# Expert tiles of 128 rows with one gather each, one summed number per list place, and earlier sums in a two-layer Flamingo block

## What is computed

```python
def _L0_ffn_ref(x, Wg, W1, W2):            # x: 4096 tokens of 128
    cap = max(1, T // E)                   # 512
    probs = jax.nn.softmax(xt @ Wg, axis=-1)
    _, top_idx = jax.lax.top_k(probs.T, cap)          # each expert takes its best 512
    ...
    tok2exp = jnp.where(assigned, jnp.argmax(masked, axis=0), jnp.argmax(pT, axis=0))
    for e in range(E):                     # each token is used by exactly one expert
        gate = jnp.where(tok2exp == e, weights, 0.0)
        out = out + gate[:, None] * (gelu(xt @ W1[e]) @ W2[e])      # 128 -> 256 -> 128
...
x = x + tanh(g_xattn[0]) * _L0_xattn_ref(_layernorm(x), ctx_1024, ctx_1024, ...)
x = x + tanh(g_ffn[0])   * _L0_ffn_ref(_layernorm(x), ...)
x = x + tanh(g_xattn[1]) * _L1_xattn_ref(_layernorm(x), ctx_1024, ...)
x = x + tanh(g_ffn[1])   * _L1_ffn_ref(_layernorm(x), ...)   # top 2 of 8, 128 -> 512 -> 128
```

## Time and profile before

| | us |
|---|---|
| median of 3 runs | 759.71 |
| lowest and highest | 758.35, 764.55 |
| the profiled execution, whole time | 760.45 |
| its span (first to last instruction) | 758.6 |
| first attention | about 0 to 216 |
| first experts: routing and list | about 216 to 275 |
| first experts: tiles | 275 to 345 |
| second attention, with its last scatters | 348 to 578 |
| second experts | 580 to 736 |
| the end | 736 to 758 |

### The profile page before, as it was taken

One profiled execution on the slowest core, in us unless ns is written; L12 is line 12 of the kernel. 1 busy time (PEld: TensorE's weight loads), 2 busy tenths in 40 slices (PEclk: granted clock), 3 DMA queues, 4 the chain that ended last, 5 costly groups with the idle time before them and its releaser, 6 DMA issues.

```text
span 758.6 us, 16969 instructions
## 1 busy us (share of the span) xinstructions
PE 539.6 (71%) x5534; PEld 435.7 (57%) x5534; DVE 502.7 (66%) x1605; ACT 358.3 (47%) x830; POOL 315.0 (42%) x439
## 2 busy tenths in 40 slices
PE   0699999998721039872699988888403999999940
PEld 0466777776510028761466756665302999999940
DVE  5568888887358862222699999998561556655625
ACT  0246777776633014330167766677402555555510
POOL 6212222221200057743755227456772455555440
PEclk9959999999955558996599999999755999999985
DMA  8443334332000004362556546241123222222229
GB/s 262 153 136 92 101 109 115 107 88 66 16 14 1 0 21 97 99 84 66 146 163 185 163 135 190 84 121 53 40 64 101 61 69 71 79 72 72 65 70 296
DMA packets 100532, 74.50 MB, mean 98 GB/s; under 512 B 12928, under 2 KB 94592, under 8 KB 100160
## 3 DMA queue, kind: packets, MB, share of 16 engines
q1 hardware_dynamic: 92336, 55.17, 25.5%
q0 software_dynamic: 7040, 14.56, 7.6%
q10 hardware_dynamic: 1072, 3.70, 1.4%
HBM read 43.64 MB, written 31.39 MB: 99 GB/s over the span
## 4 chain that ended last, share of the span: by engine, by line
PE 41%; DVE 22%; issue 11%; POOL 10%; DMA 8%; ACT 5%; SPq 2%; ACTq 1%; POOLq 0%; DVEq 0%
PE bank L943 10%; PE bank L953 10%; DVE MX L1089 7%; PE bank L740 5%; POOL PT L582 5%; PE bank L766 4%; PE bank L887 4%; PE bank L754 3%; POOL dispatched L556 3%; DVE PT L1285 2%; DMA PT<-normed,LIST 2%; PE bank L842 1%; ACT XT_HL_WR L654 1%; DMA QS_N<-MH 1%; ACT OT L678 1%
## 5 line engine op out<-in xcount | busy, mean ns | idle before, releaser
L623 ACT ACTIVATE PT<-bank 128x512 f32<-128x512 f32 x256 | 151.8, 597 | 95.1 <-PE bank L754 93.9
L1089 DVE TENSOR_REDUCE MX<-bank 128x4 f32<-128x512 f32 x256 | 172.1, 681 | 25.9 <-PE bank L766 24.2
L766 PE MATMUL bank<-KS,QS_N 96*128 96x128 f16 x1024 | 104.5, 228 | 16.7 <-DVE MX L1089 8.7
L593 POOL DMA_INDIRECT returned<-PT,META_ROW x78 | 74.9, 961 | 84.6 <-DVE PT L1403 72.4
L953 PEld LDWEIGHTS bank<-WALL,HT 128*128 128x128 f32 x808 | 100.9, 194 | 5.1 <-issue 1.7
L953 PE MATMUL bank<-WALL,HT 128*128 x808 | 102.1, 278 | 0.6 <-issue 0.6
L943 PE MATMUL bank<-XGT,XT_HL_WR 128*128 128x256 f32 x404 | 101.9, 392 | 0.0
L766 PEld LDWEIGHTS bank<-KS,QS_N 96*128 96x128 f16 x1024 | 76.6, 103 | 43.4 <-DVE MX L1089 15.3
L754 PE MATMUL bank<-QS_N,KS 98*128 98x512 f16 x256 | 98.0, 388 | 1.8 <-DMA QS_N<-MH 1.6
L943 PEld LDWEIGHTS bank<-XGT,XT_HL_WR 128*128 128x128 f32 x404 | 75.0, 198 | 8.0
L556 POOL DMA_INDIRECT dispatched<-N,SLOT x64 | 64.3, 1004 | 30.0 <-issue 14.1
(11 more groups left out here) (210 smaller groups left out, 917.4 us busy)
## 6 DMA issues: line engine op xcount, KB each, us to landing
spread<-XT_HL_WR SPq DMA_DIRECT2D x96, 128.0 KB, 2.0
QS_N<-spread SPq DMA_DIRECT2D x128, 48.0 KB
KS<-spread SPq DMA_DIRECT2D x32, 192.0 KB
PT<-dispatched SPq DMA_DIRECT2D x39, 132.0 KB, 2.1
WALL<-in_w SPq DMA_DIRECT2D x8, 578.0 KB
CT<-in_ctx SPq DMA_DIRECT2D x32, 128.0 KB
returned<-PT SPq DMA_DIRECT2D x23, 128.0 KB, 2.2
WALL<-in_w ACTq DMA_DIRECT2D x1, 2048.0 KB, 8.5
```

The lines of the kernel that those rows point to most:

```text
L593: pool.indirect_dma_start(ys[1][:, :], bass.IndirectOffsetOnAxis(ap=META_ROW[:, a.f, c:c + 1], axis=0), YS[:, a.f, c, :], None).then_inc(S ...
L623: nc.scalar.activation(PT[:, c, 4 * g:4 * g + 4, :].rearrange("p j q -> p (j q)"), ST[i % 2][:, :], ACT.Exp, scale=SCALE[layer]).then_inc( ...
L766: last = nc.tensor.matmul(MB[i % 2][:, j * P:(j + 1) * P], QS[0:96, m.r, J * g + j, c * P:(c + 1) * P], KS[0:96, m.r, g, c * P:(c + 1) * P ...
L1089: V.tensor_reduce(out=MX[:, m.u, 2 * J * g + c:2 * J * (g + 1):2], in_=MB[i % 2][:, :].rearrange("p (j k) -> p j k", j=J), op=ALU.max, axi ...
```

## The change

- The first layer's tiles have 128 slots instead of 256 (`SIZE = (P, TILE)`): 4096/128 + 7 = 39 tiles and 39 blocks. Each tile takes one gather; the same `XG` memory now is six buffers of 128 rows. Transposes, copies, products, gelu and the result's copy and write are made for 128 columns. The second layer's tiles keep 256.
- The list sums one number per place instead of two. Tokens are numbered 32 p + b, the number less 2048 fits float16, and one DVE instruction makes `IDS`; POOL's and ACT's parts and one of the two joining instructions are gone. `POS` is made in parts of 12, 8, 8 and 4 batches. A place without a token now gets 2048.
- Because tokens are numbered 32 p + b, `normed` and `returned1` are laid out in that order, and the loads at the end read 8 neighbouring rows (4096 bytes) per partition.
- In the second attention the results are gathered and added earlier: pairs 0 and 1 ahead of the slots, then by the table `GATHERS`, and added by the table `SUMS_AT` (slot, position in the slot): 1, 1, 2 and 3 pairs in slots -4 to -1, four in slot 0, four in slot 1, one in slot 2. Before it was one pair in each of the slots -4 to 11.
- `starts` compares the counts with 32 steps instead of 16, and `tables(0)` is made for 39 tiles instead of 23.

```diff
+SIZE = (P, TILE)
+TILES = (T // P + E - 1, 2 * T // TILE + E - 1)
+BLOCKS = TILES[0]
...
+PARTS = (0, 12, 20, 28, 32)
+GATHERS = {-4: (2, 3), -3: (4, 5), -2: (6, 7, 8), -1: (9, 10, 11), 0: (12, 13, 14), 1: (15,)}
+SUMS_AT = {(-4, 0): 0, (-3, 0): 1, (-2, 0): 2, (-2, 5): 3, (-1, 0): 4, (-1, 2): 5, (-1, 5): 6, (0, 1): 7, (0, 3): 8, (0, 4): 9, (0, 6): 10,
+           (1, 1): 11, (1, 2): 12, (1, 4): 13, (1, 6): 14, (2, 1): 15}
...
+    rows = (B * p + np.arange(B)[None, :]).astype(np.int32)
...
         XG = PT[:, 0].rearrange("p h q -> p (h q)")[:, 0:6 * ROW].rearrange("p (u c w) -> p u c w", u=3, c=2)
+        XG6 = XG[:, :, :, :].rearrange("p u c w -> p (u c) w")
...
-                    sp.dma_start(normed[y.b * P:(y.b + 2) * P, :].rearrange("(c p) d -> p c d", p=P),
+                    sp.dma_start(normed.rearrange("(p b) d -> p b d", b=B)[:, y.b:y.b + 2, :],
...
-                    sp.dma_start(ys[0][i * TILE:(i + 1) * TILE, :].rearrange("(c p) d -> p c d", p=P), YS[:, a.f, :, :]).then_inc(SO[a.f], 16)
+                    sp.dma_start(ys[0][i * P:(i + 1) * P, :], YS[:, a.f, 0, :]).then_inc(SO[a.f], 16)
...
-                    y = ys[1].rearrange("(b p) d -> p b d", p=P)
-                    sp.dma_start(N[:, b, 0:D], y[:, B + 8 * k:B + 8 * k + 8, :]).then_inc(YL[k], 16)
-                    sp.dma_start(N2[:, b, 0:D], y[:, b, :]).then_inc(YL[k], 16)
+                    first, second = (ys[1][T * c:T * (c + 1), :].rearrange("(p b) d -> p b d", b=B) for c in range(2))
+                    sp.dma_start(N[:, b, 0:D], second[:, b, :]).then_inc(YL[k], 16)
+                    sp.dma_start(N2[:, b, 0:D], first[:, b, :]).then_inc(YL[k], 16)
...
-                        for k in range(2 * p + 9, min(2 * p + 11, PAIRS)):
+                        for k in GATHERS[p] if p in GATHERS else ():
                             gather_results(Pair(1, k // 4, k % 4))
...
-                pool.wait_ge(own, 1)
-                nc.gpsimd.tensor_tensor(out=IDS[:, :, 1, :], in0=OWN[:, :, :], in1=const("batch").unsqueeze(2).broadcast_to([P, B, BLOCKS]),
-                                        op=ALU.mult).then_inc(ids_b, 1)
...
-                    if a.g >= 3:
-                        pool.wait_ge(xg_t, a.g - 2)
-                    for c in range(2):
-                        pool.indirect_dma_start(XG[:, a.t, c, 0:D], None, normed[:, :],
-                                                bass.IndirectOffsetOnAxis(ap=LIST[:, 2 * i + c:2 * i + c + 1], axis=0)).then_inc(XA[a.t], 16)
+                    if i >= 6:
+                        pool.wait_ge(xg_t, i - 5)
+                    pool.indirect_dma_start(XG6[:, i % 6, 0:D], None, normed[:, :],
+                                            bass.IndirectOffsetOnAxis(ap=LIST[:, i:i + 1], axis=0)).then_inc(XA[i % 6], 16)
...
-                gather_results(Pair(1, 0, 0))
+                for k in range(2):
+                    gather_results(Pair(1, 0, k))
...
-                    act.wait_ge(own, 1)
-                    nc.scalar.activation(IDS[:, :, 0, :], OWN[:, :, :], ACT.Copy, scale=const("partition")).then_inc(ids_p, 1)
...
+                        rows = (XG6[:, a.i % 6:a.i % 6 + 1, :], XG[:, a.t, :, :])[layer]
+                        for c in range(1 + layer):
+                            last = transpose(bank[4 + a.u][:, c * P:(c + 1) * P], rows[:, c, 0:D])
...
+                            n = SIZE[layer]
+                            last = nc.tensor.matmul(bank[2 * a.u + m // 2][:, n * (m % 2):n * (m % 2) + n],
+                                                    WR[:, a.t, m * P:(m + 1) * P], XGT[:, a.u, 0:n], start=True, stop=True)
...
-                        for c in range(2):
+                        for c in range(1 + layer):
                             for m in range(M):
...
+                    def add_result(u):
+                        if layer == 1 and (p, u) in SUMS_AT:
+                            k = SUMS_AT[p, u]
+                            k = Pair(1, k // 4, k % 4)
+                            dve.wait_ge(YGS[k.p % 8], 32 * (k.p // 8 + 1))
+                            for c in range(2):
+                                last = V.scalar_tensor_tensor(out=batch(k, c), in0=YG[:, k.p % 8, c, :], scalar=W0[:, k.b + c:k.b + c + 1],
+                                                              in1=batch(k, c), op0=ALU.mult, op1=ALU.add)
+                            last.then_inc(combined, 1)
...
-                    if n and layer == 1:
-                        dve.wait_ge(YGS[n.p % 8], 32 * (n.p // 8 + 1))
...
+                    add_result(0)
                     maxima(1)
                     if n:
+                        if layer == 1:
+                            dve.wait_ge(combined, n.p + 1)
...
                     routing(1)
+                    add_result(1)
                     maxima(2)
...
+                V.tensor_tensor(out=IDS[:, :, :], in0=OWN[:, :, :], in1=const("row_less_half").unsqueeze(2).broadcast_to([P, B, BLOCKS]),
+                                op=ALU.mult).then_inc(ids, 1)
+                for part in range(len(PARTS) - 1):
+                    b = slice(PARTS[part], PARTS[part + 1])
+                    n = PARTS[part + 1] - PARTS[part]
+                    V.tensor_tensor(out=POS[:, b, :], in0=const("places").unsqueeze(1).broadcast_to([P, n, P]),
+                                    in1=sm[5][:, b].unsqueeze(2).broadcast_to([P, n, P]), op=ALU.is_equal).then_inc(positions, 1)
...
-                link(V.tensor_copy(FIRST_IDS[:, :], PA[:, 0:BLOCKS]))
-                V.scalar_tensor_tensor(out=LIST[:, :], in0=PA[:, BLOCKS:2 * BLOCKS], scalar=float(P), in1=FIRST_IDS[:, :],
-                                       op0=ALU.mult, op1=ALU.add).then_inc(list_ready, 1)
+                V.tensor_scalar(out=LIST[:, :], in0=PA[:, 0:BLOCKS], scalar1=float(T // 2), scalar2=None, op0=ALU.add).then_inc(list_ready, 1)
...
-                        V.tensor_copy(YS[:, a.f, :, :].rearrange("p c d -> p (c d)"), bank[6 + a.u][:, 0:2 * D]).then_inc(y_kept, 1)
+                        V.tensor_copy(YS[:, a.f, 0, :], bank[6 + a.u][:, 0:D]).then_inc(y_kept, 1)
```

More of the change, by code:

```diff
@@ L175, in program @@
     ys = [nc.dram_tensor(f"returned{k}", [rows, D], F32, kind="Internal").ap()
-          for k, rows in enumerate((TILES[0] * TILE, PAD_ROW + T + 2 * E * TILE))]
+          for k, rows in enumerate((TILES[0] * P, PAD_ROW + T + 2 * E * TILE))]
     spread = nc.dram_tensor("spread", [2, 2, G, J, HD, 3, 2 * P], F16, kind="Internal").ap()
@@ L916, in expert_layer @@
                     rank()
-                    pe.wait_ge(ids_p, 1)
-                    pe.wait_ge(ids_b, 1)
+                    pe.wait_ge(ids, 1)
                     for b in range(B):
-                        if b % (B // 4) == 0:
-                            pe.wait_ge(positions, 4 * b // B + 1)
-                        last = nc.tensor.matmul(PA[:, 0:2 * BLOCKS], POS[:, b, :], IDS[:, b, :, :].rearrange("p k n -> p (k n)"),
-                                                start=(b == 0), stop=(b == B - 1))
+                        if b in PARTS:
+                            pe.wait_ge(positions, PARTS.index(b) + 1)
+                        last = nc.tensor.matmul(PA[:, 0:BLOCKS], POS[:, b, :], IDS[:, b, :], start=(b == 0), stop=(b == B - 1))
                     last.then_inc(listed, 1)
@@ L1334, in list_tokens @@
             def list_tokens():
[L1336 to L1338 removed]
+                slots = SLOT[:, 0, :]
+                link(V.tensor_scalar(out=CUT[:, 0, :], in0=slots, scalar1=7, scalar2=None, op0=ALU.arith_shift_right))
+                link(V.tensor_scalar(out=CUT[:, 1, :], in0=slots, scalar1=P - 1, scalar2=None, op0=ALU.bitwise_and))
@@ L1339, in list_tokens @@
                 link(V.tensor_copy(SM[:, 4:6, :], CUT[:, :, :]))
-                V.tensor_tensor(out=OWN[:, :, :], in0=const("blocks").unsqueeze(1).broadcast_to([P, B, BLOCKS]),
-                                in1=sm[4].unsqueeze(2).broadcast_to([P, B, BLOCKS]), op=ALU.is_equal).then_inc(own, 1)
-                part = B // 4
-                for k in range(4):
-                    V.tensor_tensor(out=POS[:, part * k:part * (k + 1), :], in0=const("places").unsqueeze(1).broadcast_to([P, part, P]),
-                                    in1=sm[5][:, part * k:part * (k + 1)].unsqueeze(2).broadcast_to([P, part, P]),
-                                    op=ALU.is_equal).then_inc(positions, 1)
+                link(V.tensor_tensor(out=OWN[:, :, :], in0=const("blocks").unsqueeze(1).broadcast_to([P, B, BLOCKS]),
+                                     in1=sm[4].unsqueeze(2).broadcast_to([P, B, BLOCKS]), op=ALU.is_equal))
@@ L1363, in expert_layer @@
                     link(V.tensor_copy(ex[1], PG[:, 0:E]))
-                    starts()
+                    starts(1)
                 tables(layer)
```

64 lines of the change are left out of this document (28 added, 36 removed).

## The result

The changed kernel takes **747.75 us** (median of 4 runs, 746.89 to 748.84) against 759.03 for the kernel before, a ratio of 0.9844 (95% interval 0.9818 to 0.9871). The forecast was 747, the range 741 to 756.

The account below looks back on a forecast made before the run. POOL's gathers were taken to bound the first experts, DVE the second attention, DMA the end and a DVE chain the list. From 760.45 us, -11.2 (tiles and list), -0.5 (second attention) and -1.9 (end) gave 747, range 741 to 756.

Parts of the forecast that it names:

- The sum: Whole kernel: 760.45 of the profiled execution - 11.2 - 0.5 - 1.9 = 746.9, forecast as 747; chance 0.55.
- Part 1: Making the list before the first gather: shorter `POS` and `OWN`, `IDS` on DVE, in sum -1.25 us.
- the long `POS` part: Making the list: the first part's 3659 ns against 1210 laid to POOL's share of `IDS` beside it, which goes away.
- Part 2: First-layer tiles of 128: 1.30 us per tile, stage ends at 334.2 instead of 345.4, -11.2 including Part 1.
- drain: First-layer tiles, from the last tile's transpose to the stage's end: 4.1 us instead of 6.15.
- PE's steering: First-layer tiles: semaphore instructions and register read on PE's queue set 1.30 us per tile, above arithmetic's 1.0 and POOL's 1.25.
- The fill rows' late landing: End of first-layer tiles: gathers for places without a token land by 327, PE comes at 330, so hidden.
- Part 3: Second attention, earlier gathers and sums: slot 2 about 5.1 us late, slots 3 to 11 give back 5.7, net -0.5.
- I think it can: Second attention, slots 3 to 11: PE can follow at 8.9 us per slot, giving 9 x 0.63 = -5.7.
- the rival: Second attention: slots 3 to 11 stay at 9.5 because PE sets them, 752.7 us in all; chance 0.10.
- Root 3: Second attention, slot -2: POOL issues six gathers for four ahead of this root, making it 1.85 us late.
- Part 4: The DMA-bound end: contiguous loads into `N2`, 4096-byte pieces, -1.9 us, bounds 0 and -2.9.

Follow-up runs that it names:

- pool_beside: Changed kernel, but POOL multiplies 128x1248 numbers from `OWN` into a spare place beside DVE's `POS` parts; 793.57 us, one run on chip 7.
- pe_two_reads: Changed kernel, but PE reads the register twice in every first-layer tile; 774.21 us, ratio 1.0159 to the kernel before.
- pe_no_read: Changed kernel, but DVE copies both weight matrices of a first-layer tile's expert, so PE reads no register; 744.31 us, ratio 0.9778 to the kernel before.
- old_rows: Changed kernel with the row numbers of the kernel before (128 b + p), end loads again in 512-byte pieces; 750.53 us, ratio 0.9864 to the kernel before.
- no_read_spread: Changed kernel without PE's first-layer register read, each place without a token naming its own row; 787.41 us on chip 7, ratio 0.9809.

## Why the prediction came true, step by step

**The sum** was right, and partly by luck. Against the profiled execution 13.6 was forecast and 13.6 came, with 1.76 that nobody forecast and 1.05 too few in the tiles, 1.1 in the end, 0.8 in the second attention. Against the median, 747.75, it was 0.75 off; but it had started from the profiled 760.45. From the median of the kernel before, 759.03, the same sum gives 745.4, and the gain by the medians is 11.3 and not 13.6.

**Part 1** was right in its mechanism and undersized by 0.36. `OWN` and `IDS` came within 0.05; `POS` gave 2.37 for 2.15, and PE's last part with the joining 0.72 for 0.6. The cause named for the long `POS` part holds (`pool_beside`), though it was the second part and not the first.

**Part 2** is the heart, and its steps stood. First transpose 3.43 after the first gather (3.3 forecast), tile 5's 13.62 (13.3), then 33 tiles in 43.42, 1.316 each (1.30), drain 4.35 (4.1). That PE's steering would be the bound was argued from two rounds of before and one register read; `pe_two_reads` shows it, with 0.64 us per read, and `pe_no_read` from the other side; there a tile falls by only 0.31, since at 1.00 PE's arithmetic is the bound. The fill rows' late landing was hidden as forecast. The Trainium skill (DMA: Bandwidth & Descriptors, Latency and other measured facts) gives such a load a floor of about 600 ns. This trace doesn't agree for the load itself, 297 to 367 ns. The load with the register steps behind it holds PE's queue for 640.

**Part 3** failed in one step: "I think it can", that PE would follow at 8.9 in slots 3 to 11. Three of them stayed at 9.46 to 9.49, bound by PE, which was the rival; six got shorter by 0.3 to 0.7, since they hold DVE's routing as well. All nine gave 3.4 and not 5.7. The loss ahead of them was smaller too, slot 2 came 3.3 later and not 5.1, so the net was +0.33 for -0.5 and no harm came of it. Root 3 was 1.54 late for 1.85. The error was to reason from DVE's 9.33 of 9.50 and call PE's 9.06 "stretched": 0.44 us under the slot is no proof that an engine can go faster.

**Part 4** was right in size, 1.5 over the traces for 1.9, while the one profile after showed 0.78. The rule of the Trainium skill that 512 bytes are enough for line rate (DMA: Bandwidth & Descriptors, Specifications) would give 0; `old_rows` and the fourteen traces disagree. With the shorter loads, the last store now has to wait a little for DVE's additions, one slice of 0.6 us.

**What was missing** is the first 1.76. The stretch 48 to 54 of the kernel before:

```profile
48.00:54.00 6.00, 6.00 (x57) 4.50 (x55) 3.40 (x10) 2.06 (x4) 0.93 (x2) 0.50 0.24 69
```

And of after:

```profile
48.00:54.00 6.00, 6.00 (x92) 4.63 (x95) 5.59 (x15) 3.75 (x8) 1.65 (x3) 1.00 0.27 76
```

PE was granted the lower level, 1.2 GHz, for 48 to 54 before and the higher, 2.4, after, and did 92 matmuls for 57 in the same 6 us of full work. In three traces (after, `old_rows`, `no_read_spread`) the clock of this stretch is 1.00, in the eleven others, the kernel before and ten variants of both kinds, 0.50 to 0.79. In those three the cast into `SM` starts at 261.88 to 262.17, in the others at 263.05 to 265.03. It follows none of the edits. So it is luck of one execution, and probably the larger part of the 2.3 us by which the medians lie closer together than the profiles.

## What to carry to other kernels

When tiles are halved, list what is paid per tile and not per column: register reads and semaphore instructions on the queue of the engine that will be next in line. Here it set the pace at 1.31 us over 1.00 of arithmetic, and moving the read to an engine with slack was worth 4.4 us of this stage. Work that is moved to other slots of a pipeline pays only where its engine sets the pace; read that per slot, and put it where another engine does. And before a difference of two profiles is explained, look whether the granted clock rose at the same place in both.
